# Box layer: gathers paced by the convolutions, and boxes worked out in four pieces of 16, 16, 48 and 48 rows

## The chip, the cores and the metric

One core of a Trainium2 chip. The metric is the device time of one launch in microseconds (us), the median of the runs; lower is better.

## The reference, cut to what matters

Four layers work on one image `x` of 48 x 128 x 128 numbers, each as `x = x + layer(groupnorm(x))`: attention, a patch filter, a state-space scan, and the box layer. Only the box layer is touched. It averages, for every pixel, a box of the image whose corners and divisor two small convolution nets give:

```python
integ = jnp.cumsum(jnp.cumsum(x, axis=-1), axis=-2)
h1 = gelu(_conv(x, w1_off, b1_off, 1))
sub = _conv(h1, w2_off, b2_off, 0)            # 4 offsets per pixel -> box edges
...
area = jnp.clip(area, 1.0, float(Hh * Ww))
m1 = gelu(_conv(x, w1_mod, b1_mod, 1))
area = area * _conv(m1, w2_mod, b2_mod, 0)    # 48 scales per pixel
A, Bt, Ct, D = (_grid_sample_border_bilinear(integ, corner) for corner in corners)
return (A + D - Bt - Ct) / area
```

## The kernel before, in words

Each engine (TensorE `PE`, VectorE `DVE`, ScalarE `ACT`, GpSimd `POOL`, SyncE `SP`) runs its own program in order; they meet at semaphores, written out by hand. In the box layer the 128 image rows y are handled with one image column per partition.

- `PE` writes the summed table for DRAM (`cells`), and makes 32 groups of convolutions (`convolve`, `conv3x3_split`, L182: 18 matmuls with 18 weight loads, four rows a group). `ACT` puts the Gelu over a group (`activate`, L2241), `PE` makes the heads of it (`heads_of`, L2191), `ACT` copies them to `heads` (`copy_heads`, L2247). `convolved` counts finished groups, `heads_copied` finished heads. Only when all 32 are made does `PE` begin `turn_out` (L2200), the transposes of finished rows.
- `DVE` works out the boxes 16 rows at a time (`Boxes.piece`, eight times): 20 small instructions to the cell indices, 16 to the weights, 2 to the divisor with a reciprocal. Each one waits for the one before (`then`). After the indices it raises `boxed`.
- `POOL` fetches, row by row, four indirect DMAs (L2145, 128 cells of 768 B each) into one of eight places (`GOT`); row y waits until row y-8 is weighed, and every sixteenth for `boxed`.
- `DVE` then takes each row (`row`: L2329 product, L2333 sum, L2336 divisor). `piece(p + 1)` stands after the fourth row of piece p. From row 24 on (`ADDS_FROM = 6`) two adds (`add`, L2342) stand in every group of four rows; an add waits for `turn_out`.
- `SP` writes each finished group out (L2133).

Of the kernel before, what the change touches and what calls it, by code (L numbers as in the profile page):

```python
# [23 lines left out]
ALU = mybir.AluOpType  # L24
# [4 lines left out]
C = 48  # L29
# [7 lines left out]
BLK = 512  # L37
# [3 lines left out]
class Names:  # L41


    def __init__(self, nc, ctx, tag):
        self.nc, self.ctx, self.tag = nc, ctx, tag
# [1864 lines left out]
GOT = 8  # L1910
HEAD_PIECES = NPIECE
FIRST_GROUPS = PIECE_Y // GROUP_Y
ADDS_FROM = 6
ADDS_BEHIND = 2
OUT_BANKS = 4
NTILE, PER = L // P, 4
NSUM = NTILE // PER


def box_layer(nc, image, gmean, norm, sems, ident, d, out, y_rows, skip_rows, kept_image, returned):  # L1920

# [3 lines left out]
    with ExitStack() as ctx:  # L1925
# [9 lines left out]
        b2 = n.sb("b2", [P, HEADS])  # L1935
        stats = n.sb("stats", [P, NPIX // BLK, 6])
        act1 = n.sb("act1", [SPAN, 2, BLK])
# [8 lines left out]
        got = shared[:, :].rearrange("p (s f) -> p s f", s=GOT)  # L1946
        heads = n.sb("heads", [P, HEAD_PIECES * PIECE_Y, HEADS])
        weight = n.sb("weight", [P, H, 16])
# [169 lines left out]

        def head_rows(y0, count):

            y = y0 % (HEAD_PIECES * PIECE_Y)
            return heads[:, y:y + count, :]

        @block.sync
# [11 lines left out]
        @block.gpsimd  # L2136
        def _(pool):
            for k in range(2):
                pool.wait_ge(table_stored[k], 16 * NCHUNK // 2)
            for y in range(H):  # L2140
                if y % PIECE_Y == 0:
                    pool.wait_ge(boxed, y // PIECE_Y + 1)
                wait_past(pool, weighed, y + 1 - GOT)
                for k in range(CORNERS):
                    nc.gpsimd.indirect_dma_start(  # L2145
                        got[:, y % GOT, k * CELL:(k + 1) * CELL], None, cells,
                        bass.IndirectOffsetOnAxis(index[:, k, y:y + 1], 0)).then_inc(gathered[y % GOT], 16)
# [81 lines left out]
        def _(act):  # L2229
# [14 lines left out]
            def copy_heads(i):  # L2244

                act.wait_ge(headed, i + 1)
                nc.scalar.copy(head_rows(i * GROUP_Y, GROUP_Y), ps_h[:, i % 2, 0:GROUP_Y * HEADS].rearrange(  # L2247
                    "p (y f) -> p y f", f=HEADS)).then_inc(heads_copied, 1)
# [39 lines left out]
        def _(dve):  # L2288
# [36 lines left out]
            def row(y):  # L2325
                s = y % GOT
                dve.wait_ge(gathered[s], 64 * (y // GOT + 1))
                wait_past(dve, reduced, y)
                nc.vector.tensor_tensor(prod[:, :, :], got[:, s, :].rearrange("p (k c) -> p k c", c=C),  # L2329
                                        weight[:, y, :].unsqueeze(2).broadcast_to([P, 16, C]), ALU.mult).then_inc(weighed, 1)  # L2330
                dve.wait_ge(weighed, y + 1)
                wait_past(dve, divided, y)
                nc.vector.tensor_reduce(out=total[:, :], in_=prod[:, :, :].rearrange("p k c -> p c k"), op=ALU.add,  # L2333
                                        axis=AX.X).then_inc(reduced, 1)
                dve.wait_ge(reduced, y + 1)
                nc.vector.tensor_tensor(mean[:, y, :], total[:, :], head_rows(y, 1)[:, 0, 4:HEADS],  # L2336
                                        ALU.mult).then_inc(divided, 1)
# [5 lines left out]

            def piece(p):
                dve.wait_ge(heads_copied, (p + 1) * PIECE_Y // GROUP_Y)
                box.piece(p, head_rows(p * PIECE_Y, PIECE_Y), b2, boxed)

            box = Boxes(nc, n, dve, centre, weight, index, step)
            lower(0)
# [8 lines left out]
            for k in range(2, 4):  # L2358
                for u in range(k * turns, (k + 1) * turns):
                    column(u)  # L2360
                scan_down(k)
            piece(0)
            for k in range(1, 4):
                split_low(k)
            joined = 0
            for i in range(NGROUP):
                for j in range(GROUP_Y):
                    row(i * GROUP_Y + j)
                    if j % 2 == 0 and i >= ADDS_FROM and joined <= i - ADDS_BEHIND:
                        add(joined)  # L2370
                        joined += 1
                p, first = divmod(i, PIECE_Y // GROUP_Y)
                if first == 0 and p + 1 < NPIECE:
                    piece(p + 1)
            for i in range(joined, NGROUP):
# [3 lines left out]
class Boxes:  # L2379


    def __init__(self, nc, n, dve, centre, weight, index, step):
        self.nc, self.dve, self.centre, self.weight, self.index, self.step = nc, dve, centre, weight, index, step
        self.count = 0
        r = PIECE_Y
        self.mean = n.sb("x_mean", [P, r, 2])
        self.dev = n.sb("x_dev", [P, 2, r, 2])
        self.edge = n.sb("x_edge", [P, r, 2, 2])
        self.pos = n.sb("x_pos", [P, r, 2, 2])
        self.whole = n.sb("x_whole", [P, r, 2, 2], I32)  # L2390
        self.cell = n.sb("x_cell", [P, r, 2, 2])
        self.above = n.sb("x_above", [P, r, 2, 2])
        self.part = n.sb("x_part", [P, r, 2, 2, 2])
        self.size = n.sb("x_size", [P, r, 2])
        self.area = n.sb("x_area", [P, r])

# [5 lines left out]

    def piece(self, p, heads, b2, boxed):

        nc, then = self.nc, self.then
        mean, dev, edge, pos, whole, cell, above, part, size, area = (
            self.mean, self.dev, self.edge, self.pos, self.whole, self.cell, self.above, self.part, self.size, self.area)
        rows = slice(p * PIECE_Y, (p + 1) * PIECE_Y)
        tt, ts, stt = nc.vector.tensor_tensor, nc.vector.tensor_scalar, nc.vector.scalar_tensor_tensor
        flat = lambda t: t[:, :, :, :].rearrange("p y a e -> p (y a e)")  # L2410
        ends = lambda t, e: t[:, :, :, e]
        off = heads[:, :, 0:4].rearrange("p y (a e) -> p y a e", e=2)

        then(tt(heads, heads, b2[:, :].unsqueeze(1).broadcast_to([P, PIECE_Y, HEADS]), ALU.add))
        then(tt(mean[:, :, :], off[:, :, :, 0], off[:, :, :, 1], ALU.add))
        then(ts(mean[:, :, :], mean[:, :, :], 0.5, None, ALU.mult))
        for e in range(2):
            then(tt(dev[:, e, :, :], off[:, :, :, e], mean[:, :, :], ALU.subtract))
        then(stt(out=ends(edge, 0), in0=dev[:, 0, :, :], scalar=-MIN_OFFSET, in1=dev[:, 1, :, :],
                 op0=ALU.min, op1=ALU.min))  # L2420
        then(stt(out=ends(edge, 1), in0=dev[:, 0, :, :], scalar=MIN_OFFSET, in1=dev[:, 1, :, :],
                 op0=ALU.max, op1=ALU.max))

        then(tt(pos[:, :, :, :].rearrange("p y a e -> p (y a) e"), edge[:, :, :, :].rearrange("p y a e -> p (y a) e"),
                self.centre[:, rows, :].rearrange("p y a -> p (y a)").unsqueeze(2).broadcast_to([P, 2 * PIECE_Y, 2]), ALU.add))
        then(ts(flat(pos), flat(pos), -1.0, 1.0, ALU.max, ALU.min))
# [8 lines left out]
        for ey in range(2):  # L2435
            for ex in range(2):
                then(stt(out=self.index[:, ey * 2 + ex, rows], in0=cell[:, :, 0, ex], scalar=float(H),  # L2437
                         in1=cell[:, :, 1, ey], op0=ALU.mult, op1=ALU.add))
        self.dve.sem_inc(boxed, 1)

        fraction = above
        then(tt(flat(fraction), flat(pos), flat(cell), ALU.subtract))
        then(ts(part[:, :, :, 0, 0], ends(fraction, 0), -1.0, None, ALU.add))
        then(ts(part[:, :, :, 0, 1], ends(fraction, 0), -1.0, None, ALU.mult))
        then(ts(part[:, :, :, 1, 0], ends(fraction, 1), -1.0, 1.0, ALU.mult, ALU.add))
        then(nc.vector.tensor_copy(part[:, :, :, 1, 1], ends(fraction, 1)))
        for ey in range(2):
            for dy in range(2):
                dst = self.weight[:, rows, 8 * ey:8 * ey + 8].rearrange("p y (e b s) -> p y e b s", b=2, s=2)
                for ex in range(2):  # L2450
                    then(tt(dst[:, :, ex, dy, :], part[:, :, 0, ex, :],  # L2451
                            part[:, :, 1, ey, dy:dy + 1].broadcast_to([P, PIECE_Y, 2]), ALU.mult))
        then(tt(size[:, :, :], ends(edge, 1), ends(edge, 0), ALU.subtract))
        then(stt(out=area[:, :], in0=size[:, :, 1], scalar=AREA, in1=size[:, :, 0], op0=ALU.mult, op1=ALU.mult))
        then(ts(area[:, :], area[:, :], 1.0, float(NPIX), ALU.max, ALU.min))
        scales = heads[:, :, 4:HEADS]
        then(tt(scales, scales, area[:, :].unsqueeze(2).broadcast_to([P, PIECE_Y, C]), ALU.mult))  # L2457
        then(nc.vector.reciprocal(scales, scales))  # L2458

# [118 lines left out]
def program(nc, d, out):  # L2578

    with ExitStack() as ctx:  # L2580
# [19 lines left out]
        rows = scan_layer(nc, image, gmean, norm, sems, ident, d, stats, kept_image, kept)  # L2600
        box_layer(nc, image, gmean, norm, sems, ident, d, out, *rows)

# [13 lines left out]
```

## Time and profile before

| | |
|---|---|
| median of 3 runs | 7519.23 us (7515.94 to 7521.47) |
| the profiled execution: its time, its span | 7518.81 us, 7517.1 us |
| box layer's gathers, first to last | 6699.06 to 7507.19 us from the span's start |
| last group of convolutions starts | 6963.63 us |
| granted TensorE clock, mean | 0.937 |

Times in rows are microseconds from the span's start. A timeline row gives start, duration, engine, line, operation, output <- inputs, shapes, count, and in brackets the idle time before it and what ended it. "issue" is idle time in which the profile shows nothing that was waited for; "remote" is an event of no engine shown.

### The profile page before, as it was taken

The numbers are of one execution on the slowest core, as the hardware profiler recorded it, in microseconds if no ns is written. First come the engines' busy times: TensorE is split into PE (matmuls) and PEld (weight loads), VectorE is DVE, ScalarE is ACT, GpSimd is POOL, SyncE is SP. The second block draws the span as 40 slices with busy tenths as digits, with TensorE's granted clock in tenths as the row PEclk, the third lists the DMA queues.
The fourth block names the chain that finished last, engine by engine and source line by source line (L and its number), as shares of the span: only waits on it lengthen the run. The fifth ranks groups of instructions, "written<-read, shape, count | busy, mean of one in ns | idle before, by whom it ended". The sixth has DMA issues, their size and how long they took to land. (4 is left out here: it accounts for less than half of the span.)

```text
span 7517.1 us, 169527 instructions
## 1 busy us (share of the span) xinstructions
PE 6082.4 (81%) x69188; PEld 2639.6 (35%) x69188; DVE 6727.2 (89%) x6038; ACT 5237.8 (70%) x5319; POOL 3441.3 (46%) x1801
## 2 busy tenths in 40 slices
PE   6899999999999999897688888888888888765100
PEld 3433333333333333564233333333333333343000
DVE  8899999999999999797799999999999999863666
ACT  3488888888888888333588888888888888620000
POOL 2000000000000000000499999999999999744666
PEclk9999999999999999998899999999999999976555
DMA  3200000000000000000200000000000000121222
GB/s 66 56 12 10 9 9 11 10 10 9 9 12 9 10 9 6 8 6 11 71 6 6 6 6 6 6 6 6 6 6 6 6 6 6 32 82 47 66 74 76
DMA packets 146946, 153.67 MB, mean 20 GB/s; under 512 B 66540, under 2 KB 125708, under 8 KB 144924
## 3 DMA queue, kind: packets, MB, share of 16 engines
q1 hardware_dynamic: 120224, 89.43, 4.6%
q0 software_dynamic: 24576, 50.36, 2.6%
q8 instruction: 529, 8.67, 0.5%
q10 hardware_dynamic: 1440, 3.75, 0.3%
q14 instruction: 177, 1.45, 0.1%
HBM read 101.83 MB, written 37.95 MB: 19 GB/s over the span
## 5 line engine op out<-in xcount | busy, mean ns | idle before, releaser
L1891 POOL TENSOR_TENSOR k_image<-k_image,s_b 128x1024 f32<-128x1024 f32 x1152 | 2702.6, 2357 | 117.1 <-ACT k_image L1804 83.4
L797 ACT ACTIVATE att_prob<-att_scores,a_bound,a_temp 128x1024 f32<-128x1024 f32 x2048 | 2356.7, 1202 | 361.8 <-PE att_scores L747 361.8
L808 DVE TENSOR_TENSOR att_prob_lo<-att_prob 128x1024 f16<-128x1024 f32 x2048 | 2440.1, 1238 | 169.2 <-ACT att_prob L797 158.8
L732 POOL TENSOR_TENSOR k_image<-k_image,att_rden 48x512 f32 x32 | 68.6, 2143 | 2893.5 <-DVE att_rden L829 2893.5
L1804 ACT COPY k_image<-h_du 128x1024 f32<-128x1024 f32 x1152 | 1166.4, 1013 | 322.8 <-PE h_du L1738 322.4
L1854 DVE TENSOR_TENSOR_SCAN h_state_odd<-h_keep,k_image 128x1024 f32<-128x1024 f32 x576 | 1321.9, 2332 | 0.3 <-ACT h_keep L1810 0.3
L1810 ACT ACTIVATE h_keep<-h_keep,h_decay 128x1024 f32<-128x1024 f32 x1152 | 1256.7, 1091 | 75.2 <-PE h_keep L1727 51.4
L747 PE MATMUL att_scores<-att_queries,att_keys 32*128 32x512 f16 (+1 forms) x20480 | 1292.9, 377 | 19.7 <-DMA att_keys<-qk_halves 17.0
L764 PE MATMUL att_sums<-att_prob,a_values 128*64 128x512 bf16 x8192 | 1129.2, 396 | 0.0
L1727 PE MATMUL h_keep<-h_rows,h_spread 128*128 128x512 bf16 x2304 | 699.5, 385 | 511.0 <-DVE h_state_odd L1854 263.2
L1738 PE MATMUL h_du<-h_rows,h_spread 128*128 128x512 bf16 x2304 | 701.2, 386 | 35.8 <-DMA h_rows<-parts 33.5
L747 PEld LDWEIGHTS att_scores<-att_queries,att_keys 32*128 32x128 f16 (+1 forms) x20480 | 436.7, 93 | 792.1 <-ACT att_prob L797 408.6
L2145 POOL DMA_INDIRECT b_shared<-cells,b_index x512 | 509.6, 995 | 370.3 <-issue 151.6
L1854 DVE TENSOR_TENSOR_SCAN k_image<-h_keep,h_state_odd,k_image 128x1024 f32<-128x1024 f32 x288 | 660.9, 2332 | 0.0
L1854 DVE TENSOR_TENSOR_SCAN k_image<-h_keep,k_image 128x1024 f32<-128x1024 f32 x288 | 643.5, 2271 | 8.3 <-POOL k_image L1891 7.3
L771 PE MATMUL att_sums<-att_prob_lo,a_values 128*64 128x512 f16 x4096 | 610.7, 378 | 0.0
L764 PEld LDWEIGHTS att_sums<-att_prob,a_values 128*64 128x64 f16 x8192 | 371.3, 108 | 671.2 <-ACT att_prob L797 408.0
L1727 PEld LDWEIGHTS h_keep<-h_rows,h_spread 128*128 128x128 bf16 x2304 | 133.4, 97 | 1075.7 <-DVE h_state_odd L1854 488.3
L2200 PE MATMUL b_ps_o<-k_ident,b_passed 128*48 128x128 f32 x128 | 30.6, 395 | 513.5 <-DVE b_passed L2336 433.2
L1756 PE MATMUL h_y<-h_state_odd,s_c 128*32 128x192 f32 x4096 | 324.6, 336 | 1.8 <-DVE h_state_odd L1854 1.8
L1756 PE MATMUL h_y<-k_image,s_c 128*32 128x192 f32 x4096 | 324.0, 336 | 0.0
L771 PEld LDWEIGHTS att_sums<-att_prob_lo,a_values 128*64 128x64 f16 x4096 | 226.2, 109 | 246.7 <-DVE att_prob_lo L808 0.3
(309 smaller groups left out, 6454.0 us busy)
## 6 DMA issues: line engine op xcount, KB each, us to landing
y_rows<-h_y_sb SPq DMA_DIRECT2D x1024, 3.0 KB
att_queries<-qk_halves SPq DMA_DIRECT2D x124, 128.0 KB, 2.2
parts<-t_part SPq DMA_DIRECT2D x48, 192.0 KB, 2.5
h_rows<-parts SPq DMA_DIRECT2D x128, 72.0 KB
b_shared<-cells,b_index POOLq DMA_INDIRECT x512
qk_halves<-qkv_hi SPq DMA_DIRECT2D x128, 48.0 KB, 1.6
cells<-b_shared SPq DMA_DIRECT2D x4, 1536.0 KB, 5.1
att_keys<-qk_halves SPq DMA_DIRECT2D x32, 128.0 KB, 2.9
```

Source lines behind the costliest of these rows:

```text
L747: last = nc.tensor.matmul(scores[:, (2 * n + r // 2) % SLOTS_S, r % 2 * BLK:(r % 2 + 1) * BLK], keys[part, j, g * KT:(g + 1) * KT], querie ...
L764: nc.tensor.matmul(sums[part, slot, :], values[:, key_tile(u, r), part], prob_hi[:, u % RING, r * BLK:(r + 1) * BLK], start=g == 0 and r = ...
L771: last = nc.tensor.matmul(sums[r * CHUNK:(r + 1) * CHUNK, slot, :], values[:, key_tile(u, r), 0:CHUNK], prob_lo[:, u % RING, r * BLK:(r + ...
L797: nc.scalar.activation(prob[:, u % RING, :], scores[:, u % SLOTS_S, :], ACT.Exp, bias=bound[:, 0:1], scale=temp[:, 0:1]).then_inc(prob_rea ...
L808: nc.vector.tensor_tensor(prob_lo[:, u % RING, :], prob[:, u % RING, :], prob_hi[:, u % RING, :], ALU.subtract).then_inc(low_ready, 1)
L1727: last = nc.tensor.matmul(keep[:, k % 2, cols], spread[:, 0, slot, :], rows[:, c % 2, cols], start=True, stop=True)
L1738: last = nc.tensor.matmul(du[:, cols], spread[:, 1, slot, :], rows[:, c % 2, cols], start=True, stop=True)
L1756: last = nc.tensor.matmul(out, b_c[stat][:, c * CH + t0:c * CH + t0 + TB], h[:, s0:s0 + d1 - d0, t0:t0 + TB], start=stat == 2, stop=stat == 4)
L1804: nc.scalar.copy(du_sb[k % 3], du[:, :]).then_inc(du_copied, 1)
L1810: nc.scalar.activation(keep[:, k % 2, :], keep[:, k % 2, :], ACT.Exp, scale=decay[:, ds(g * SLOTS + k // STEPS * SLOTS + k % SLOTS, 1)]).t ...
L1854: nc.vector.tensor_tensor_scan(out=state[c % 2][:, slot, :], data0=keep[:, k % 2, :], data1=drive[k % 3], initial=initial, op0=ALU.mult, o ...
L1891: nc.gpsimd.tensor_tensor(drive[k % 3], du_sb[k % 3], b[:, c * CH:(c + 1) * CH], ALU.mult).then_inc(drive_ready, 1)
```

## The change

1. `POOL`: row 0 is fetched once the first boxes are there. Row y, for y = 1 to 12, also waits until 8 + 2y groups are convolved, so row 12 waits for all 32. Later rows are free.
2. Boxes come in four pieces, `BOX_ROWS`: rows 0-15, 16-31, 32-79, 80-127. `piece` is split into `indices` (20 instructions, raises `boxed`), `weights` (16) and `scales` (3: the bias add of the 48 scales is now apart). `scales` stays at 16 rows, eight times.
3. Where they stand on `DVE`, by groups of four rows i: `indices(1)` and `weights(1)` after i = 0, `indices(2)` after 3, `weights(2)` after 4, `indices(3)` after 5, `weights(3)` after 7, `scales(p + 1)` after the third group of piece p.
4. `ADDS_FROM` is 5: adds begin at row 20.
5. Memory: `stats` is the tile of the layers before; some tiles share a place; `heads` is indexed plainly.

```diff
-HEAD_PIECES = NPIECE
-ADDS_FROM = 6
+ADDS_FROM = 5
 ADDS_BEHIND = 2
+BOX_ROWS = ((0, PIECE_Y), (PIECE_Y, 2 * PIECE_Y), (2 * PIECE_Y, 5 * PIECE_Y), (5 * PIECE_Y, H))
+AHEAD_GROUPS = 2 * PIECE_Y // GROUP_Y
+GROUPS_PER_ROW = 2
...
             for y in range(H):
-                if y % PIECE_Y == 0:
-                    pool.wait_ge(boxed, y // PIECE_Y + 1)
+                for k, (first, _) in enumerate(BOX_ROWS):
+                    if y == first:
+                        pool.wait_ge(boxed, k + 1)
+                if 0 < y <= (NGROUP - AHEAD_GROUPS) // GROUPS_PER_ROW:
+                    pool.wait_ge(convolved, AHEAD_GROUPS + GROUPS_PER_ROW * y)
                 wait_past(pool, weighed, y + 1 - GOT)
...
-            def piece(p):
-                dve.wait_ge(heads_copied, (p + 1) * PIECE_Y // GROUP_Y)
-                box.piece(p, head_rows(p * PIECE_Y, PIECE_Y), b2, boxed)
+            def indices(k):
+                y0, y1 = BOX_ROWS[k]
+                dve.wait_ge(heads_copied, y1 // GROUP_Y)
+                box.indices(y0, y1)
...
-            piece(0)
+            indices(0)
+            box.weights(*BOX_ROWS[0])
+            box.scales(0)
...
-                p, first = divmod(i, PIECE_Y // GROUP_Y)
-                if first == 0 and p + 1 < NPIECE:
-                    piece(p + 1)
+                if i == 0:
+                    indices(1)
+                    box.weights(*BOX_ROWS[1])
+                if i == 3:
+                    indices(2)
+                if i == 4:
+                    box.weights(*BOX_ROWS[2])
+                if i == 5:
+                    indices(3)
+                if i == 7:
+                    box.weights(*BOX_ROWS[3])
+                p, turn = divmod(i, PIECE_Y // GROUP_Y)
+                if turn == 2 and p + 1 < NPIECE:
+                    box.scales(p + 1)
...
+    def scales(self, p):
+
+        rows = slice(p * PIECE_Y, (p + 1) * PIECE_Y)
+        tt = self.nc.vector.tensor_tensor
+        scales = self.heads[:, rows, 4:HEADS]
+        self.then(tt(scales, scales, self.b2[:, 4:HEADS].unsqueeze(1).broadcast_to([P, PIECE_Y, C]), ALU.add))
+        self.then(tt(scales, scales, self.area[:, rows].unsqueeze(2).broadcast_to([P, PIECE_Y, C]), ALU.mult))
+        self.then(self.nc.vector.reciprocal(scales, scales))
```

## Rows read from the trace of the kernel before

**Rows 1.** The page: span.
```profile
span 7517.1 us, 169527 instructions
```

**Rows 2.** Waits from 6700 to the end: in total, times, longest.
```profile
PEld b_ps_c L182 <- issue: 101.8, 67, 3.3
...
POOL b_shared L2145 <- DVE b_prod L2329: 147.3, 12, 64.7
...
DVE k_image L2342 <- PE b_ps_o L2200: 76.1, 2, 75.7
...
ACT b_act L2241 <- remote: 56.2, 4, 32.6
```

**Rows 3.** Windows of PE: length, busy and count, clock, DMA share, GB/s.
```profile
6707.00:6739.00 32.00, 28.88 (x148) 0.95 0.20 55
6739.00:6862.00 123.00, 23.70 (x51) 0.51 0.27 71
6862.00:6897.00 35.00, 31.72 (x158) 0.88 0.12 31
6897.00:6911.00 14.00, 4.80 (x15) 0.65 0.25 67
6911.00:6970.00 59.00, 58.96 (x320) 0.97 0.00 1
```

**Rows 4.** Timeline of PE: convolutions at full pace, and one matmul between.
```profile
6717.65 4.06 PE L182 MATMUL b_ps_c<-b_x_split,b_w_split 112*112 112x512 f16 x18
...
6722.38 4.06 PE L182 MATMUL b_ps_c<-b_x_split,b_w_split 112*112 112x512 f16 x18
...
6757.96 0.59 PE L182 MATMUL b_ps_c<-b_x_split,b_w_split 112*112 112x512 f16 x1 [2.21 <-issue]
...
6963.63 4.06 PE L182 MATMUL b_ps_c<-b_x_split,b_w_split 112*112 112x512 f16 x18
```

**Rows 5.** DMA queues in 6871 to 6872: packets, MB, share of 16 engines.
```profile
q8 instruction: 1, 0.02, 6.0%
```

**Rows 6.** Timeline of POOL: the first gather, three after a wait, the last.
```profile
6699.06 1.17 POOL L2145 DMA_INDIRECT b_shared<-cells,b_index  x1 [70.87 <-DVEq L2439]
...
6882.56 0.95 POOL L2145 DMA_INDIRECT b_shared<-cells,b_index  x1 [30.13 <-DVE b_prod L2329]
...
6972.08 0.95 POOL L2145 DMA_INDIRECT b_shared<-cells,b_index  x1 [64.70 <-DVE b_prod L2329]
...
7131.82 0.94 POOL L2145 DMA_INDIRECT b_shared<-cells,b_index  x1 [18.90 <-DVE b_prod L2329]
...
7507.19 0.95 POOL L2145 DMA_INDIRECT b_shared<-cells,b_index  x1 [0.30 <-issue]
```

**Rows 7.** Windows of the gathers alone (L2145), columns as in rows 3.
```profile
7131.80:7213.00 81.20, 61.49 (x64) 0.50 0.31 81
6780.20:6807.10 26.90, 20.80 (x20) 0.50 0.28 73
```

**Rows 8.** Timeline of DVE: row products, and index instructions fed well and badly.
```profile
6784.07 0.95 DVE L2329 TENSOR_TENSOR b_prod<-b_shared,b_weight 128x768 f32<-128x768 f32 x1
...
6788.28 0.95 DVE L2329 TENSOR_TENSOR b_prod<-b_shared,b_weight 128x768 f32<-128x768 f32 x1
...
6793.16 0.95 DVE L2329 TENSOR_TENSOR b_prod<-b_shared,b_weight 128x768 f32<-128x768 f32 x1
...
7008.13 0.90 DVE L2437 SCALAR_TENSOR_TENSOR b_index<-b_x_cell 128x16 uint32<-128x16 f32 x4
...
7111.39 0.19 DVE L2437 SCALAR_TENSOR_TENSOR b_index<-b_x_cell 128x16 uint32<-128x16 f32 x1 [1.21 <-DVE b_index L2437]
...
7454.67 0.96 DVE L2329 TENSOR_TENSOR b_prod<-b_shared,b_weight 128x768 f32<-128x768 f32 x1 [2.35 <-DMA b_shared<-cells,b_index]
...
7509.77 0.96 DVE L2329 TENSOR_TENSOR b_prod<-b_shared,b_weight 128x768 f32<-128x768 f32 x1 [2.25 <-DMA b_shared<-cells,b_index]
```

**Rows 9.** The reciprocal of a piece, grouped by line and form.
```profile
L2458 DVE RECIPROCAL b_heads<-b_heads 128x768 f32<-128x768 f32 x8 | 39.6, 4953 | 1.9 <-DVE b_heads L2457 1.8
```

More of the change, by code:

```diff
@@ L1917, with box_layer @@
 NSUM = NTILE // PER
-def box_layer(nc, image, gmean, norm, sems, ident, d, out, y_rows, skip_rows, kept_image, returned):
+def box_layer(nc, image, gmean, norm, sems, ident, d, stats, out, y_rows, skip_rows, kept_image, returned):
     cells = nc.dram_tensor("cells", [NPIX, PAIR_ROW], F32, kind="Internal").ap()
@@ L1935, in box_layer @@
         b2 = n.sb("b2", [P, HEADS])
-        stats = n.sb("stats", [P, NPIX // BLK, 6])
         act1 = n.sb("act1", [SPAN, 2, BLK])
@@ L1946, in box_layer @@
         got = shared[:, :].rearrange("p (s f) -> p s f", s=GOT)
-        heads = n.sb("heads", [P, HEAD_PIECES * PIECE_Y, HEADS])
+        heads = n.sb("heads", [P, H, HEADS])
         weight = n.sb("weight", [P, H, 16])
@@ L2117, in box_layer @@
         parts = C * CHUNK_Y // BLK
-        def head_rows(y0, count):
-            y = y0 % (HEAD_PIECES * PIECE_Y)
-            return heads[:, y:y + count, :]
         @block.sync
@@ L2246, in copy_heads @@
                 act.wait_ge(headed, i + 1)
-                nc.scalar.copy(head_rows(i * GROUP_Y, GROUP_Y), ps_h[:, i % 2, 0:GROUP_Y * HEADS].rearrange(
+                nc.scalar.copy(heads[:, i * GROUP_Y:(i + 1) * GROUP_Y, :], ps_h[:, i % 2, 0:GROUP_Y * HEADS].rearrange(
                     "p (y f) -> p y f", f=HEADS)).then_inc(heads_copied, 1)
@@ L2335, in row @@
                 dve.wait_ge(reduced, y + 1)
-                nc.vector.tensor_tensor(mean[:, y, :], total[:, :], head_rows(y, 1)[:, 0, 4:HEADS],
+                nc.vector.tensor_tensor(mean[:, y, :], total[:, :], heads[:, y, 4:HEADS],
                                         ALU.mult).then_inc(divided, 1)
@@ L2342, in add @@
                 nc.vector.tensor_tensor(image[HI, px], ps_o[0:C, i % OUT_BANKS, :], image[HI, px], ALU.add).then_inc(added, 1)
-            def piece(p):
-                dve.wait_ge(heads_copied, (p + 1) * PIECE_Y // GROUP_Y)
-                box.piece(p, head_rows(p * PIECE_Y, PIECE_Y), b2, boxed)
-            box = Boxes(nc, n, dve, centre, weight, index, step)
+            def indices(k):
+                y0, y1 = BOX_ROWS[k]
+                dve.wait_ge(heads_copied, y1 // GROUP_Y)
+                box.indices(y0, y1)
+            box = Boxes(nc, n, dve, heads, b2, centre, weight, index, boxed, step)
             lower(0)
@@ L2379, with __init__ @@
 class Boxes:
-    def __init__(self, nc, n, dve, centre, weight, index, step):
-        self.nc, self.dve, self.centre, self.weight, self.index, self.step = nc, dve, centre, weight, index, step
+    def __init__(self, nc, n, dve, heads, b2, centre, weight, index, boxed, step):
+        self.nc, self.dve, self.heads, self.b2, self.centre, self.weight, self.index, self.boxed, self.step = (
+            nc, dve, heads, b2, centre, weight, index, boxed, step)
         self.count = 0
-        r = PIECE_Y
-        self.mean = n.sb("x_mean", [P, r, 2])
-        self.dev = n.sb("x_dev", [P, 2, r, 2])
+        r = max(last - first for first, last in BOX_ROWS)
         self.edge = n.sb("x_edge", [P, r, 2, 2])
         self.pos = n.sb("x_pos", [P, r, 2, 2])
+        self.cell = n.sb("x_cell", [P, r, 2, 2])
+        self.mean = self.size = n.sb("x_mean", [P, r, 2])
+        middle = n.sb("x_middle", [P, 4 * r])
+        self.dev = middle[:, :].rearrange("p (e y a) -> p e y a", e=2, a=2)
+        self.above = middle[:, :].rearrange("p (y a e) -> p y a e", a=2, e=2)
         self.whole = n.sb("x_whole", [P, r, 2, 2], I32)
-        self.cell = n.sb("x_cell", [P, r, 2, 2])
-        self.above = n.sb("x_above", [P, r, 2, 2])
         self.part = n.sb("x_part", [P, r, 2, 2, 2])
-        self.size = n.sb("x_size", [P, r, 2])
-        self.area = n.sb("x_area", [P, r])
+        self.area = n.sb("x_area", [P, H])
     def then(self, ins):
@@ L2401, in then @@
         self.dve.wait_ge(self.step, self.count)
[L2403 to L2408, printed above, removed]
-        tt, ts, stt = nc.vector.tensor_tensor, nc.vector.tensor_scalar, nc.vector.scalar_tensor_tensor
[L2410 to L2416, printed above, removed]
-        for e in range(2):
[L2418 to L2425, printed above, removed]
@@ new lines, in indices @@
+    def indices(self, y0, y1):
+        nc, then, r = self.nc, self.then, y1 - y0
+        mean, dev, edge, pos, whole, cell, above = (self.mean[:, 0:r], self.dev[:, :, 0:r], self.edge[:, 0:r],
+                                                    self.pos[:, 0:r], self.whole[:, 0:r], self.cell[:, 0:r], self.above[:, 0:r])
+        rows = slice(y0, y1)
+        tt, ts, stt = nc.vector.tensor_tensor, nc.vector.tensor_scalar, nc.vector.scalar_tensor_tensor
+        flat = lambda t: t.rearrange("p y a e -> p (y a e)")
+        offsets = self.heads[:, rows, 0:4]
+        off = offsets.rearrange("p y (a e) -> p y a e", e=2)
+        then(tt(offsets, offsets, self.b2[:, 0:4].unsqueeze(1).broadcast_to([P, r, 4]), ALU.add))
+        then(tt(mean, off[:, :, :, 0], off[:, :, :, 1], ALU.add))
+        then(ts(mean, mean, 0.5, None, ALU.mult))
+        for e in range(2):
+            then(tt(dev[:, e], off[:, :, :, e], mean, ALU.subtract))
+        then(stt(out=edge[:, :, :, 0], in0=dev[:, 0], scalar=-MIN_OFFSET, in1=dev[:, 1], op0=ALU.min, op1=ALU.min))
+        then(stt(out=edge[:, :, :, 1], in0=dev[:, 0], scalar=MIN_OFFSET, in1=dev[:, 1], op0=ALU.max, op1=ALU.max))
+        then(tt(pos.rearrange("p y a e -> p (y a) e"), edge.rearrange("p y a e -> p (y a) e"),
+                self.centre[:, rows, :].rearrange("p y a -> p (y a)").unsqueeze(2).broadcast_to([P, 2 * r, 2]), ALU.add))
@@ L2438, in piece, with weights @@
                          in1=cell[:, :, 1, ey], op0=ALU.mult, op1=ALU.add))
-        self.dve.sem_inc(boxed, 1)
-        fraction = above
+        self.dve.sem_inc(self.boxed, 1)
+    def weights(self, y0, y1):
+        nc, then, r = self.nc, self.then, y1 - y0
+        edge, pos, cell, fraction, part, size = (self.edge[:, 0:r], self.pos[:, 0:r], self.cell[:, 0:r], self.above[:, 0:r],
+                                                 self.part[:, 0:r], self.size[:, 0:r])
+        rows = slice(y0, y1)
+        area = self.area[:, rows]
+        tt, ts, stt = nc.vector.tensor_tensor, nc.vector.tensor_scalar, nc.vector.scalar_tensor_tensor
+        flat = lambda t: t.rearrange("p y a e -> p (y a e)")
         then(tt(flat(fraction), flat(pos), flat(cell), ALU.subtract))
[L2443 to L2446, printed above, removed]
+        then(ts(part[:, :, :, 0, 0], fraction[:, :, :, 0], -1.0, None, ALU.add))
+        then(ts(part[:, :, :, 0, 1], fraction[:, :, :, 0], -1.0, None, ALU.mult))
+        then(ts(part[:, :, :, 1, 0], fraction[:, :, :, 1], -1.0, 1.0, ALU.mult, ALU.add))
+        then(nc.vector.tensor_copy(part[:, :, :, 1, 1], fraction[:, :, :, 1]))
         for ey in range(2):
@@ L2451, in piece @@
                     then(tt(dst[:, :, ex, dy, :], part[:, :, 0, ex, :],
[L2452 to L2458, printed above, removed]
+                            part[:, :, 1, ey, dy:dy + 1].broadcast_to([P, r, 2]), ALU.mult))
+        then(tt(size, edge[:, :, :, 1], edge[:, :, :, 0], ALU.subtract))
+        then(stt(out=area, in0=size[:, :, 1], scalar=AREA, in1=size[:, :, 0], op0=ALU.mult, op1=ALU.mult))
+        then(ts(area, area, 1.0, float(NPIX), ALU.max, ALU.min))
+    def scales(self, p):
[5 more added lines that the diff above has]
+        self.then(self.nc.vector.reciprocal(scales, scales))
 def real_fourier(m=PATCH):
@@ L2600, in program @@
         rows = scan_layer(nc, image, gmean, norm, sems, ident, d, stats, kept_image, kept)
-        box_layer(nc, image, gmean, norm, sems, ident, d, out, *rows)
+        box_layer(nc, image, gmean, norm, sems, ident, d, stats, out, *rows)
 def kernel(**inputs):
```

## The prediction

> **What bounds the kernel now.** I read the page first, then the waits of the last 800 us, then windows and timeline of the stretches that the waits point to. The change touches the box layer alone; everything before its first gather at 6699.06 stays. From there to the end of the span at 7517.1 [rows 1, 6] POOL has to issue 512 gathers, four for each of 128 rows, and DVE, PE and ACT have far less than 818 us of work. So the question is when POOL stood still, and why.
>
> At its own pace POOL is regular. Products of DVE, once DVE keeps up and takes each row as it lands, stand at 7454.67 and 7509.77 with 11 rows between them: 55.10 / 11 = 5.01 us a row, 1.252 a gather [rows 8]. 128 rows of that are 641 us. The remaining 177 us are what a change can win. The waits give them: POOL waited 147.3 us for a place that DVE had not emptied [rows 2], of it 30.13 until 6882.56 and 64.70 until 6972.08, and the other 52.5 behind those, the largest 18.90 [rows 6]. The rest is gathers that take longer than 1.252.
>
> Why was DVE late? Three stretches answer. (a) Until 6970 it stood 75.7 us in its first add, which waits for `turn_out`, and that stands on PE behind all 32 groups of convolutions [rows 2]. The last group starts only at 6963.63 [rows 4]. (b) PE was not short of data: it waited 101.8 us before weight loads of convolutions for "issue", that is for nothing that the profile shows, and ACT 56.2 us for "remote" [rows 2]. By windows PE is busy 28.88 of 32 us until 6739, then 23.70 of 123 us, then 31.72 of 35, 4.80 of 14, and 58.96 of 59 when no gather runs [rows 3]. In the slow stretch single matmuls stand 2.8 us apart (0.59 and an idle 2.21) [rows 4], and by the windows the clock is the lower one (0.51, 1.2 GHz) and the DMA engines are 27% busy [rows 3]. (c) DVE has the same illness: four index instructions take 0.90 us together when fed well, and later come one by one: 0.19 of work behind 1.21 of idle, 1.40 a piece (7111.39) [rows 8]. What all three engines share is their instruction queues. One such packet of 16 KB (0.02 MB) takes 0.96 us when no gather runs (6.0% of 16 engines in 1 us) [rows 5]. I read the slow stretches as a block of instructions that comes in drop by drop between the packets of gathers. That it is the gathers fits the times: PE recovers at 6862, when POOL has stood still since 6852.4 (6882.56 less its 30.13), and starves again at 6897, 14 us after POOL resumes [rows 3, 6].
>
> The Trainium skill, "Runtime: NRT & Kernel Launch", section "Instruction fetch mechanics", says that an engine fetches its next 16 KiB block by a DMA queue of its own while it executes the current one, at a cost that is mostly hidden. The size agrees with the 0.02 MB packet; the hiding does not agree with 101.8 us of "issue". By that rule as it stands the slow stretches would not be loading at all, which is the second rival below.
>
> **Part 1, the pace on rows 1 to 12.** Start: PE runs a group in 4.73 us when fed (6717.65 to 6722.38) [rows 4]. From the group at 6717.65, number 8, to the last, number 31, are 23 groups. 23 x 4.73 = 108.8, so group 31 starts at 6826.4 and ends at 6830.5 with its 4.06 [rows 4]. In the old kernel this end came at 6967.7, so 137 us of PE are given back. POOL pays with rows: by 6830.5 it has issued only rows 0 to 11, where the old one had fetched 33 rows by 6972.08, its 65 us wait included. What is queued behind the new wait on POOL is only the later gathers; behind late rows waits DVE, which has nothing else due.
>
> Does PE stay fed while 11 bursts of four gathers run? A burst lasts 5 us, then 4.4 us are quiet. No row shows this pattern. Lower bound of the cost: nothing, since PE ran 14 us at full pace with gathers running (6882.56 to 6897) [rows 3, 6]. Upper bound: PE falls to the starved pace in every burst. It loses 1 - 23.70/123 = 81% of 5 us, 11 times: 44 us. I take 5, close to the lower bound, because a burst is a third of those 14 us and the quiet after it is longer than a block's 0.96.
>
> **Part 2, fewer box instructions.** 8 x 38 = 304 become 4 x 36 + 8 x 3 = 168. Fed badly, each is 1.40 us [rows 8], so DVE loses up to 190 us of drip-fed work, and the 52.5 us that POOL waited after 6972 should mostly go. But the pieces for rows 32 to 127 now crowd between rows 16 and 31: 2 x 36 instructions and one `scales`. Worst, all starved: 75 x 1.40 = 105 us and 16 rows at 4.21 us (6784.07 to 6788.28) [rows 8] = 67, and the reciprocal's 4.95 [rows 9]: 177 us. POOL needs 16 x 5.01 = 80 for the same rows and is 7 rows, 35 us, ahead: up to 62 us of waiting. Against it stand a block loaded while POOL was held (DVE has little to do then), and that a POOL that stops feeds DVE at once: the waits of this kind in the old kernel were 19 us at most. Bounds 0 and 62; I take 4, since the work at 7008.13 shows that well-fed DVE does a whole piece in the time of a few gathers. Wider instructions (192 numbers for 64) I put at nothing: DVE is not the bound here, and if each cost twice its 0.2 us, that would be 72 x 0.2 = 14 us on DVE beside 80 of POOL. The extra bias add is one instruction per 16 rows, hidden the same way. The earlier adds (row 20) cost nothing: row 20 is fetched some 40 us after the last convolution, and `turn_out` has long been free. The 75.7 us of (a) go with it. The tiles' new places issue nothing.
>
> **Part 3, POOL from row 12 on.** 116 rows are 464 gathers, 463 steps. Bounds: 1.252 each (DVE keeps up), 580 us; or 26.90 / 20 = 1.345 (DVE behind and drip-fed), 623 us [rows 7]. Between them lie 64 gathers in 81.2 us, 1.269 [rows 7]. I take that, 587.5 us, the state after a piece, since DVE is behind for only part of the way. The tail from the last gather to the end is 7517.1 - 7507.19 = 9.9 us and stays [rows 1, 6].
>
> **The sum.** 6830.5 + 5 + 587.5 + 4 + 9.9 = 7436.9 us of span, against 7517.1. The profiled execution's time is 1.7 us over its span, and the median shown is 0.4 over that time: 7439.0, so **7439 us**, 1.1% less.
>
> **The rivals.**
> 1. *DVE's instructions run short in rows 16 to 31.* The upper bound of part 2 in part: POOL waits 20 to 40 us more. For it: 2 x 36 instructions between 16 rows. Against: the block held in store. 7459 to 7479. Chance 0.14.
> 2. *Every burst slows PE at once*, with nothing held in store: the 44 us in place of 5, so 7478. This is what would hold if loading were hidden and the gathers slowed the engines some other way. The skill's rule named above would lead here, by 7478 as against 7439. Against it: the 14 us at full pace. Chance 0.08.
> 3. *Without pauses DVE never recovers, and becomes the bound.* The old kernel gave DVE a quick refill in each pause of POOL; now 116 rows run without one. If a row costs 4.88 us starved (6788.28 to 6793.16) [rows 8], with a quarter of an add (0.35) and a sixteenth of `scales` (4.20 + 4.95, 0.57), DVE needs 5.8 us a row: 116 x 5.8 = 673 in place of 587, so 7525: no faster, or slower. It decides from (7517.1 - 7436.9 + 587.5) / 116 = 5.76 us a row. Against it: at 4.21 for the row the sum is 5.1, level with POOL, and the last dozen rows before the end ran at 5.01 with DVE waiting for data each time. Chance 0.08, over half of it slower.
> 4. *The held rows cost more than the convolutions give.* Needs the last group to end after 6830.5 + 5 + 80.2 = 6916, that is a loss of 85 us in bursts, twice the upper bound. Chance 0.03.
>
> **How the numbers follow.** My forecast's case has 0.67; its own range is 7422 (no loss on PE, no wait, 1.252 a gather: 6830.5 + 580 + 9.9 + 2.1 = 7422) to 7459. The range reaches over rivals 1 and 2 to 7492. Of the forecast, rival 1 and 2 all is faster; so is a small part of 3. Change of 0.2%, 15 us, is about what a measurement of this kernel can tell from no change. Faster 0.90, within 0.2% 0.04, slower 0.06.
>
> **What would show it.** The last convolution starts near 6826 to 6835, with PE over 0.85 busy from 6707 on and hardly any "issue" before L182; far more "issue" there in steps of 4 us per burst is rival 2. POOL waits for PE between rows 1 and 12, and for DVE under 20 us in all after; more, with box instructions 1.4 us apart just before, is rival 1. DVE waits for gathers in most rows behind row 32; if instead POOL waits for DVE evenly to the end, it is rival 3. The prediction is wrong above all if PE starves between bursts.

## The result: 0.5% faster, half of the forecast gain

| | before | after |
|---|---|---|
| median of 5 runs each | 7521.47 us (7515.94 to 7526.14) | 7483.13 us (7479.81 to 7486.23) |
| ratio, 95% interval | | 0.9949 [0.9938, 0.996] |
| profiled execution: time, span | 7518.81, 7517.1 us | 7483.13, 7471.9 us |
| time outside the span | 1.7 us | 11.2 us |

The time lies inside the forecast range and on the forecast side, but 44.1 us over 7439. The page and the waits of the stretch from 6690 on, of the kernel after, against [rows 1, 2]; lines stand one to a few places from those of before (gathers L2144, product L2328).

```profile
span 7471.9 us, 169388 instructions
```

```profile
DVE b_prod L2328 <- DMA b_shared<-cells,b_index: 238.3, 83, 9.2
...
POOL b_shared L2144 <- PE b_ps_c L182: 75.1, 12, 22.8
...
POOL b_shared L2144 <- DVE b_prod L2328: 11.3, 1, 11.3
...
PEld b_ps_c L182 <- issue: 1.7, 8, 0.2
```

PE's unexplained waits before convolutions are gone (1.7 us for 101.8), POOL's wait for DVE is 11.3 us for 147.3, and DVE now waits 238.3 us for gathers, in 83 rows. So 136 us of POOL waiting went, and the convolutions are done at 6832, not at 6968. Yet the time fell by 38 us. First PE while the rows are held (columns: length, busy us and count, granted clock, DMA share, GB/s), against [rows 3]:

```profile
6707.00:6832.00 125.00, 125.00 (x676) 0.98 0.13 35
```

PE is busy for all of the 125 us of the hold, at the 2.4 GHz level (0.98). Now POOL's own timeline: the first gathers of image rows 1, 2 and 12, two of the late stretch, and the last:

```profile
6728.65 0.94 POOL L2144 DMA_INDIRECT b_shared<-cells,b_index  x1 [22.82 <-PE b_ps_c L182]
...
6738.10 0.94 POOL L2144 DMA_INDIRECT b_shared<-cells,b_index  x1 [4.75 <-PE b_ps_c L182]
...
6832.56 1.25 POOL L2144 DMA_INDIRECT b_shared<-cells,b_index  x1 [4.76 <-PE b_ps_c L182]
...
7331.37 1.09 POOL L2144 DMA_INDIRECT b_shared<-cells,b_index  x1 [0.30 <-issue]
7335.57 1.79 POOL L2144 DMA_INDIRECT b_shared<-cells,b_index  x1 [0.31 <-issue]
...
7455.77 0.95 POOL L2144 DMA_INDIRECT b_shared<-cells,b_index  x1 [0.30 <-issue]
```

Row 12 begins 2.9 us ahead of the forecast 6835.5. But from there to the last gather are 623.2 us, not 591.5 (587.5 and a wait of 4). The windows of the gathers tell when:

```profile
7050.00:7100.00 50.00, 38.12 (x40) 0.50 0.31 82
7300.00:7400.00 100.00, 76.02 (x71) 0.50 0.28 74
```

40 gathers in 50 us are 1.25 each; 71 in 100 are 1.41. No wait is named in the late stretch, and the idle 0.30 ahead of a gather is the usual one for all but 5 of the 71. What has grown is some of the gathers' own rows: 44 of the 71 take 0.94 to 0.96 us as ever, the other 27 take 0.99 to 1.80, and the mean is 1.07 (76.02 / 71) where it was 0.95 (38.12 / 40). POOL slows near 7200 and stays slow. The end is different as well. The drain that ends POOL's program (L1927; durations in ns, then the start), and two late rows of DVE:

```profile
L1927 POOLq DRAIN  x1: 22738/22738/22738, 7448.7 to 7448.7; - x1
```

```profile
7458.45 0.96 DVE L2328 TENSOR_TENSOR b_prod<-b_shared,b_weight 128x768 f32<-128x768 f32 x1 [2.42 <-DMA b_shared<-cells,b_index]
...
7462.27 0.68 DVE L2341 TENSOR_TENSOR k_image<-b_ps_o,k_image 48x512 f32<-48x512 f32 x1 [0.43 <-PE b_ps_o L2199]
```

The last gather is issued at 7455.77 and its data are used at 7458.45, 2.7 us later, as in the old kernel (7507.19 to 7509.77). DVE is done at 7463. But POOL's drain ends at 7471.4 (7448.7 + 22.7), and another 11.2 us follow outside the span. The profiled time ends some 25 us after the last data have landed. Nothing moves from 7465 to 7472 (DMA share 0.00). After that the DMA queues carry only blocks of instructions, until just before the time ends (queue and kind, packets, MB, share of 16 engines, from 7465 to 7484):

```profile
q14 instruction: 8, 0.07, 1.2%
q8 instruction: 2, 0.03, 0.8%
```

So what runs behind the span is, as far as the profile shows, the loading of instructions, and in this kernel it takes 11.2 us.

### The profile page after: what moved, and what is told of

Same layout as the page of the kernel before. It is cut to its first block and busy times, and to the rows that moved or that the text cites. A ratio compares the mean times of both kernels' runs of the same rounds, so it can differ in the third digit from the quotient of the medians.

```text
span 7471.9 us, 169388 instructions
## 1 busy us (share of the span) xinstructions
PE 6062.0 (81%) x69188; PEld 2635.0 (35%) x69188; DVE 6709.0 (90%) x5902; ACT 5234.7 (70%) x5319; POOL 3445.5 (46%) x1801
## 5 line engine op out<-in xcount | busy, mean ns | idle before, releaser
L1854 DVE TENSOR_TENSOR_SCAN h_state_odd<-h_keep,k_image 128x1024 f32<-128x1024 f32 x576 | 1363.1, 2461 | 0.3 <-ACT h_keep L1810 0.3
L1854 DVE TENSOR_TENSOR_SCAN k_image<-h_keep,h_state_odd,k_image 128x1024 f32<-128x1024 f32 x288 | 681.5, 2461 | 0.0
L1854 DVE TENSOR_TENSOR_SCAN k_image<-h_keep,k_image 128x1024 f32<-128x1024 f32 x288 | 663.3, 2396 | 7.8 <-POOL k_image L1891 7.0
L2144 POOL DMA_INDIRECT b_shared<-cells,b_index x512 | 515.2, 1006 | 311.3 <-issue 154.9
L2328 DVE TENSOR_TENSOR b_prod<-b_shared,b_weight 128x768 f32<-128x768 f32 x128 | 123.0, 961 | 252.8 <-DMA b_shared<-cells,b_index 238.3
L1864 DVE TENSOR_TENSOR k_image<-h_y,h_diagonal 128x384 f32<-128x384 f32 x512 | 338.1, 660 | 8.8 <-PE h_y L1756 8.7
```

The source lines that it names most:

```text
L1854: nc.vector.tensor_tensor_scan(out=state[c % 2][:, slot, :], data0=keep[:, k % 2, :], data1=drive[k % 3], initial=initial, op0=ALU.mult, o ...
L2144: nc.gpsimd.indirect_dma_start(got[:, y % GOT, k * CELL:(k + 1) * CELL], None, cells, bass.IndirectOffsetOnAxis(index[:, k, y:y + 1], 0)). ...
```

## The experiments

Of what slowed POOL late there were these ideas: its own instructions come in slowly (as I had read PE and DVE); DVE's work beside it; the bytes or pieces moved; or a fixed cost per gather behind POOL, with a store in front of it that fills up. The old kernel was timed again beside each group of runs, and its medians came out from 7520.2 to 7532.3. The changed kernels hardly drifted with it (e4 at 7484.3 beside an old kernel of 7532.3, e5 at 7483.8 beside 7520.4), so a difference of 0.2% between ratios can be the old kernel's alone; where that matters, the bare times are given too.

**e1_hold_only**: the old kernel with the hold alone.

```diff
+                if 0 < y <= 12:
+                    pool.wait_ge(convolved, 8 + 2 * y)
```

> The kernel before with the hold on rows 1 to 12 alone; boxes stay in eight pieces, adds start at row 24. Theory A (the prediction's mechanism for the convolutions, and a GpSimd that is short of its own instructions once it never pauses): row 12 is fetched near 6832 as in the changed kernel; the old pauses for boxes stay (six of about 12 us, 70 us in all) but gathers between them keep 1.25 to 1.29 us, so the last gather comes near 7490 and the time is 7495 to 7515. Rival B (gathers stretched by VectorE's work whatever the pauses): 7515 to 7535, with gathers at 1.35 or more late in the layer.

Measured: 7506.57 us, ratio 0.9965 [0.9953, 0.9978], as theory A had it. POOL waits 76.0 us for DVE, 11 times, up to 24.0, and mostly issues at 1.25 to 1.28 between.

**e2_boxes_only**: the new kernel without the hold.

```diff
-                if 0 < y <= (NGROUP - AHEAD_GROUPS) // GROUPS_PER_ROW:
-                    pool.wait_ge(convolved, AHEAD_GROUPS + GROUPS_PER_ROW * y)
```

> The changed kernel without the hold: rows 1 to 12 are free. Theory A: the convolutions starve as before and end near 6960 to 6970, VectorE stands in its first add until then and GpSimd stops after row 28. From there 99 rows at 1.27 rising to 1.40 us a gather: 7500 to 7540, so no gain. Rival (the pieces alone carry the gain): below 7490.

Measured: 7509.34 us, 0.997 [0.9959, 0.9982], inside theory A's range. PE starves as in the old kernel, 76.8 us of "issue", and the late pace is 1.37 (waits, then the window of its gathers, L2142):

```profile
POOL b_shared L2142 <- DVE b_prod L2326: 99.5, 7, 57.3
...
PEld b_ps_c L182 <- issue: 76.8, 67, 3.3
```

```profile
7300.00:7400.00 100.00, 76.33 (x73) 0.50 0.29 77
```

Each half alone is faster than before. The slow pace comes where POOL has long gone without a pause, hold or no hold.

**e3_pauses**: the new kernel, POOL pausing every 16 rows until DVE has caught up, so that all engines could refill.

```diff
+                if y >= 28 and y % 16 == 12:
+                    pool.wait_ge(weighed, y)
```

> The changed kernel, but at rows 28, 44, 60, 76, 92, 108 and 124 GpSimd also waits until the row before is weighed, a pause of about 2.4 us each, 17 us in all. Theory A (GpSimd's own instructions load drop by drop while it gathers, and a pause lets the rest of the block in): the gathers after 7170, 1.37 to 1.42 us in the changed kernel, go back to about 1.26, which saves 25 to 30 us, so the time is 8 to 15 us shorter, 7468 to 7476. Rival B (VectorE's work stretches them): gathers stay at 1.40 late, and the pauses are added: 7495 to 7503.

Measured: 7496.85 us, 0.9953 [0.9936, 0.9969]. Theory A's 7468 to 7476 missed. The time lies in rival B's 7495 to 7503, and the late pace did not recover, as B had it; B's cause, DVE's work, is what e5 takes away. The ratio is that of the change, but the bare time is 12.5 us above e4, which ran in the same group, and 13.7 above the change itself: the pauses cost something (the account below has 16 us). POOL's waits for DVE are 47.2 us in place of 11.3, of them 26.2 in one wait until 6939 and 20.4 in six of 3.4, so less than half of what was added shows in the time. Over the 80 us from 7340, one pause of 3.4 included, 57 gathers were issued, 1.40 each as without pauses. That speaks against slow instructions, which a pause should mend, and for a bound behind POOL that works on through a pause.

**e4_pad**: two more waits on a count long reached, written ahead of every second gather. The trace has one instruction more for each such pair, 230 in all: two a row, as the expectation counts them.

```diff
+                    if y > 12 and k % 2:
+                        pool.wait_ge(boxed, 1)
+                        pool.wait_ge(boxed, 1)
```

> The changed kernel with two more instructions a row on GpSimd for rows 13 to 127 (waits on a count long reached; 230 in all, 10 in place of 8 a row), nothing else. Theory A: late gathers go from 1.40 to about 1.75 us (10 instructions of 0.70 us per four gathers) and the short supply begins earlier, so 40 to 120 us longer: 7523 to 7600. Rival B: a satisfied wait costs some tens of ns, 230 of them at most 15 us: 7483 to 7498.

Measured: 7484.3 us, 0.9934 [0.9918, 0.9951], in rival B's range and far from theory A's. With more instructions the late pace is no slower: 74 gathers in the 100 us from 7300, and 72 in those from 7350. POOL's own instructions aren't what is short.

**e5_little_dve**: product and sum on 48 of the 768 numbers of a row; the output is then one product in place of the sum over 16.

```diff
-                nc.vector.tensor_tensor(prod[:, :, :], got[:, s, :].rearrange("p (k c) -> p k c", c=C),
+                nc.vector.tensor_tensor(prod[:, 0:1, :], got[:, s, 0:C].rearrange("p (k c) -> p k c", c=C),
```

> The changed kernel, but VectorE multiplies and sums only the first 48 of 768 numbers of a row (the other 15 of 16 products are left out). Theory C, formed from the first runs: something behind GpSimd serves one gather in 1.40 us whatever GpSimd issues (1.25), about 18 gathers can wait for it, after that GpSimd is held to 1.40, and at the end the store has to empty; 464 gathers x 1.40 = 650 us after 6832 set the end. Then this run is as the changed kernel, 7475 to 7492 where the kernel before has 7521, late gathers at 1.39 to 1.42 us. Theory D (VectorE's products and sums block GpSimd's writes): late gathers at 1.25 to 1.27, 30 to 45 us shorter, 7438 to 7453.

**e6_half_bytes**: 384 B for each index, not 768. **e7_half_rows**: 64 indices per gather, not 128. Both leave out half of the data and so work on wrong numbers.

```diff
-                        got[:, y % GOT, k * CELL:(k + 1) * CELL], None, cells,
+                        got[:, y % GOT, k * CELL:k * CELL + PAIR_ROW], None, cells,
```

```diff
-                        got[:, y % GOT, k * CELL:(k + 1) * CELL], None, cells,
-                        bass.IndirectOffsetOnAxis(index[:, k, y:y + 1], 0)).then_inc(gathered[y % GOT], 16)
+                        got[0:64, y % GOT, k * CELL:(k + 1) * CELL], None, cells,
+                        bass.IndirectOffsetOnAxis(index[0:64, k, y:y + 1], 0)).then_inc(gathered[y % GOT], 16)
```

> The changed kernel with 384 B fetched for each index in place of 768 (one of the two neighbouring table cells, so half of each corner's numbers are old ones). 128 pieces a gather as before. If the 1.40 us of theory C is bytes or DMA time, it halves, GpSimd's own 1.25 sets the pace, and the time is 7425 to 7450 on a scale where the kernel before has 7521. If it goes by pieces or by gathers: as the changed kernel, 7475 to 7492. Theory D: no change either.

> The changed kernel with gathers of 64 pieces (partitions 0 to 63; the other half keeps old numbers), still 512 of them. If theory C's 1.40 us goes by pieces: 0.70 us a gather, and GpSimd's issue sets the pace; the span after 6832 shrinks to 464 x the issue step, at most 580 us, time 7200 to 7440. If it is a fixed cost of one gather: late gathers still 1.40 and the time as the changed kernel's, even where GpSimd could issue faster.

Measured: 7483.83, 7483.22 and 7487.8 us; 0.995 [0.9933, 0.9966], 0.995 [0.9934, 0.9967] and 0.9957 [0.994, 0.9974]. All three stand within 5 us of the change, as a fixed cost per gather would have it. The same window of the gathers, e5, e6, e7 in turn:

```profile
7300.00:7400.00 100.00, 76.35 (x72) 0.50 0.28 74
```

```profile
7300.00:7400.00 100.00, 78.14 (x72) 0.50 0.18 39
```

```profile
7300.00:7400.00 100.00, 76.48 (x72) 0.50 0.17 39
```

72 gathers each time, at 74 or 39 GB/s. Neither DVE, bytes nor pieces set the late pace; what is left of these ideas is a cost per gather of about 1.40 us.

**e10_three**: three gathers a row, the fourth corner left out, so 384 gathers in all.

```diff
-                for k in range(CORNERS):
+                for k in range(CORNERS - 1):
```

> The changed kernel with three gathers a row in place of four (the fourth corner keeps old numbers). Theory C, a fixed 1.40 us for each gather: 348 gathers after 6832 are 487 us, 7319 to 7335; up to 20 more if VectorE, at 4.2 us a row, falls behind. If the cost goes with rows or with time on other engines in place of gathers: above 7400.

This too works on wrong numbers. Measured: 7339.52 us, 0.9744 [0.9728, 0.976], in the expected range with its allowance for DVE. That is 144 us under the changed kernel's 7483 (by the ratios, 154). The 116 gathers less behind the hold would be 162 us at 1.40 and 145 at 1.25. POOL now waits for DVE nine times, 31 us, and DVE's last rows run back to back up to 7334, 11 us past the last gather, so that DVE's rows and not the gathers set the end. The run can't tell 1.40 from 1.25; it only bounds the cost per gather from below.

**e8_pace, e9_dense, e11_early, e12_full**: the hold denser, so that more rows are fetched beside the convolutions.

```diff
-                if 0 < y <= (NGROUP - AHEAD_GROUPS) // GROUPS_PER_ROW:
-                    pool.wait_ge(convolved, AHEAD_GROUPS + GROUPS_PER_ROW * y)
+                if 0 < y <= 16:                                  # e8_pace
+                    pool.wait_ge(convolved, 8 + (3 * y + 1) // 2)
+                if 0 < y <= 20:                                  # e9_dense
+                    pool.wait_ge(convolved, 7 + (5 * y + 3) // 4)
+                if 0 < y <= 17:                                  # e11_early
+                    pool.wait_ge(convolved, 6 + (3 * y + 1) // 2)
+                if 0 < y <= 22:                                  # e12_full
+                    pool.wait_ge(convolved, 5 + (6 * y + 4) // 5)
```

> The changed kernel with one row per one and a half groups held back, rows 1 to 16 in place of 1 to 12 (row y waits for 8 + 1.5y groups, rounded up). A burst of 5 us then comes every 7.1 us. Theory C: four rows less remain after the last convolution, 16 x 1.40 = 22 us shorter, 7458 to 7466 where the kernel before has 7521, if the convolutions still end near 6832. Rival (convolutions starve when bursts stand that close): they end 20 us or more later, and the time is 7480 to 7500.

> The changed kernel with 20 rows paced: row y waits for 7 + 1.25y groups, rounded up, so a row of four gathers every 5.9 us, for which theory C's server needs 5.6 us. If the convolutions still end near 6832, 108 rows remain, 432 x 1.40 = 605 us, and the time is 7434 to 7442 where the kernel before has 7521. Second statement of theory C: instructions load only while the server has nothing waiting, so with 0.3 us of rest in 5.9 the convolutions may starve; then they end by 6840 to 6880 and the time is 7445 to 7485, and PE shows issue waits before L182. Either way the time minus the end of the convolutions is 605 us.

> The changed kernel with row y held for 6 + 1.5y groups, rounded up: rows 1 to 17, the first burst 9.4 us earlier than in the changed kernel, one row more than with 8 + 1.5y. Theory C: 444 or 440 gathers remain after 6832, so 7451 to 7457, 5.6 us below the 7459 of that run. Rival: the early bursts meet VectorE's long subtractions (4.4 us each until 6722), which hold GpSimd up, and nothing is won: 7457 to 7463.

> The changed kernel with 22 rows paced: row y waits for 5 + 1.2y groups, rounded up, a row every 5.67 us where theory C's server needs 5.6. If the convolutions still end near 6832, 106 rows remain, 424 x 1.40 = 594 us, and the time is 7425 to 7433 where the kernel before has 7521. If a load of 99% no longer lets the blocks of instructions through, TensorE waits for issue before L182, the convolutions end at 6845 or later, and the time is 7440 or more.

| | groups per row (row 1 waits for) | 4 x 1.40 us as a share | us | ratio |
|---|---|---|---|---|
| after | 2 (10) | 0.59 | 7483.13 | 0.9949 [0.9938, 0.996] |
| e8_pace | 1.5 (10) | 0.79 | 7459.07 | 0.9919 [0.9902, 0.9936] |
| e11_early | 1.5 (8) | 0.79 | 7455.28 | 0.9898 [0.9881, 0.9914] |
| e9_dense | 1.25 (9) | 0.95 | **7440.78** | **0.9879 [0.9862, 0.9895]** |
| e12_full | 1.2 (7) | 0.99 | 7442.79 | 0.9896 [0.9879, 0.9912] |

The share is 5.6 us of gathers over the time of that many groups at 4.73 us. The expectations of e8, e9 and e11 were worked out from 1.40 us a gather before these runs, and all three times fall inside them; e12's fell where it was to fall if PE starves. PE in the hold, e9_dense:

```profile
6707.00:6832.00 125.00, 125.00 (x672) 0.98 0.21 58
```

and e12_full, windows, then waits:

```profile
6707.00:6832.00 125.00, 114.51 (x594) 0.93 0.22 58
```

```profile
PEld b_ps_c L182 <- issue: 17.7, 37, 1.9
```

At a share of 0.95 PE loses nothing. At 0.99 it starves again, in part (13.11 us busy of the 20 from 6740), and the last group starts at 6848.68 against 6828.20 in e9_dense. e12_full also starts its gathers two groups earlier, and no run parts the two, so that the share is the reason is likely and not shown. e9_dense is the best version found, 1.1 to 1.2% faster than before by bare times and by the ratio; e12_full is 2 us behind it, which these few runs hardly tell apart.

## Why the forecast gain came only by half

Take it that each gather, behind POOL, is finished at the later of its own start and the finish before it, plus 1.40 us. The 1.40 is read from the late pace; nothing else is fitted. (With 0.01 us more per gather the times worked out would be up to 5 us longer.) Over the start times of all gathers in each trace the last finish is, beside the profiled execution's time:

| | worked out | profiled |
|---|---|---|
| before | 7518.6 | 7518.8 |
| after | 7484.2 | 7483.1 |
| e1, e2, e3 | 7504.7, 7509.3, 7500.6 | 7505.3, 7509.1, 7496.2 |
| e4, e5 | 7487.9, 7485.4 | 7487.3, 7485.3 |
| e6, e7 | 7483.1, 7484.2 | 7481.9, 7484.0 |
| e8, e11 | 7459.4, 7456.2 | 7457.4, 7454.1 |
| e9, e12 | 7442.2, 7447.5 | 7439.5, 7444.6 |
| e10 (384 gathers) | 7328.7 | 7339.8 |

All but e10 come within 5 us. By the same account 10 gathers at most are unfinished at once in the old kernel. In the new one they are 17 and more from about 7190 on and 21 at 7304, where POOL has fallen to 1.40, and the most in e2 to e9, e11 and e12 is 19.4 to 20.4: a store of about 20. In the old kernel every wait for DVE let the store empty, and that is why its pace was 1.25 to the end. The 512 gathers are 716.8 us of that service in any kernel; what a schedule can win is only the time in which nothing is being served: 102.7 us before (7518.6 - 6699.06 - 716.8), 67.2 after, 25.9 in e9_dense. The first difference is 35.5 us, and the profiled times differ by 35.7. What the account meets is the time and not the end of the span: in the change the last instructions come in behind the span, and that ends at 7483 where the account has the store empty at 7484.2.

Now the steps of the prediction. That 7483 lies in its range is luck: the range reached up to 7492 for rivals 1 and 2, and neither is what happened. The miss is -2.9 (row 12's first gather) + 31.7 (463 steps) + 6.2 (tail of the span) + 9.1 (outside it) = 44.1 us.

- **Part 1, right in its times.** The last group was to end at 6830.5 and ends at 6832.3 (6828.23 + 4.06). The 5 us for bursts were 0. Rivals 2 and 4 did not come: their condition, PE starving in each burst, is refuted by 125.00 of 125 us.
- **Part 2, nearly right.** One wait of POOL for DVE, 11.3 us in place of 4, inside the bounds of 0 and 62. That is rival 1 at a third of its price. By the account it cost less than it looks, as the store was being served for all but 1.9 us of it.
- **Part 3 is the step that failed.** "Between them lie 64 gathers in 81.2 us, 1.269 [rows 7]. I take that": 463 steps measured 611.9 us besides the wait, 1.32 on the mean, 1.25 to 1.3 early and 1.40 late. I had read 1.25 as what a gather costs once DVE keeps up, and the 1.345 of [rows 7] as DVE being behind. 1.25 is only what POOL needs to hand one over; the layer pays 1.40. The upper bound, 623, held the value, with a wrong reason: DVE was not behind. What made 1.345 in the old kernel, where the store was never full by the account, stays open.
- **"The tail ... stays"** failed with it: 16.1 us and 11.2 outside the span, where I had 9.9 and 2.1. Tail and pace are one thing: 6832.56 + 464 x 1.40 = 7482.2 gives the time of 7483.1 with no tail at all.
- **The 52.5 us that POOL waited after 6972** I counted as won. They were not the bound: by the account only 14.5 us of that time were idle behind POOL. e1 alone, with 76.0 us of such waits left, is 0.9965, and taking them away too brings only 0.9949.
- **Rival 3, no.** DVE kept up (238.3 us of waits for gathers), though only the one pause came; at 5.6 us a row it has time left.

Of the reading of the starved stretches one half stands: it is the gathers that starve PE, and what counts is less whether POOL issues than whether gathers are unfinished behind it. In the old kernel POOL's last gather before its wait starts at 6851.48, the account is empty at 6864.9, and PE's idle before convolutions ends at 6862.3, 2.6 us ahead of that; after the burst to 6906.43 it is empty at 6910.6, and PE is at full pace from 6910.7. It isn't at once: PE ran 14 us unhurt from 6882.56 on, and all through e9_dense. The other half, a block of instructions that comes in drop by drop, is not shown. The instruction packets of the old kernel from 6740 to 6862, and the first line of those of the change from 6707 to 6832:

```profile
q14 instruction: 1, 0.01, 0.0%
```

```profile
q8 instruction: 5, 0.08, 0.3%
```

Queue q8 brings five blocks in 125 us while PE runs its convolutions at full pace, and none in 122 us while PE starves; the next is the one of [rows 5], after POOL has stopped. What PE got drop by drop in those 122 us came in no packet of that queue that the profile shows. One number is worth keeping: a starved instruction takes 1.40 us on DVE and 1.40 on PE (a weight load and a matmul in 2.80) [rows 8, 4], and a gather is served in 1.40. No run here says why they agree. The Trainium skill, "Runtime: NRT & Kernel Launch", section "Instruction fetch mechanics", has loading mostly hidden; e12_full's 17.7 us of "issue" beside the 1.7 of the change, with the same PE program, does not agree with it, if that idle time is loading.

What it is that takes 1.40 us is open. It isn't the transfer of the data: half the bytes change nothing, and the last data are used 2.7 us after issue even with some 20 gathers unfinished by the account. The account is worked out, not seen: no view shows the store, only what fits it (the late pace, POOL's long drain, the late loading at the end).

## What to carry to other kernels

Price a queue by two numbers, what the engine needs to issue one and what stands behind it needs to serve one, and read the second only where the issue has run long without a pause; a busy share or a pace after pauses gives the first. If a pause of the issuing engine goes away and the time stays, look at the end of the program, where a store has to empty. Spread such work evenly under other work up to just below its full load (0.95 was free here), since every four gathers moved there take 5.6 us off the end (eight rows in e9_dense: 44.8 worked out, 43.6 between the profiled times).

## What the runs showed of the hardware that was not expected

- An indirect gather from POOL costs about 1.40 us in a long run, the same with 128 pieces of 768 B, 128 of 384 B or 64 of 768 B, while POOL can issue one each 1.25. The rows of its gathers show 0.95 us while it isn't held back. The Trainium skill, "Perfetto Trace Analysis", section "DMA Instruction — SWDGE (GPSIMD)", says that such a row ends when the descriptors are written and not when the data have moved; the trace agrees (a row of 0.95 us, data used after 2.7).
- POOL's drain ended 13.0 us after the last data began to be used, and the program's time ran on for 11.2 us behind the span, with nothing but ten instruction packets; before it was 4.3 (7514.1 - 7509.77) and 1.7.
- PE ran unhurt beside gathers at 0.95 of that rate (2.5 us of "issue" before its convolutions in e9_dense) and lost 17.7 us at 0.99 (e12_full). That what it lacks is instructions is inferred from the idle time having no other cause in the profile.
